# Front's masks on row halves, local scores as fp32 products without DRAM, and the last batch's networks by halves, under a new static order

## What is computed

```python
scores = jnp.einsum('bhqd,bhkd->bhqk', q, k) * scale       # Front: heads of 8, q and k rotated
attn = softmax(scores + causal_mask);  out = attn @ v @ Wo.T
...
gate = fp4_linear(x, w_gate);  y = fp4_linear(x, w_up)      # ffn: 128 -> 352 -> 128
return fp4_linear(silu(gate) * y, w_down)                   # both operands quantised in blocks of 16
...
att = jnp.einsum('bghqd,bghkd->bghqk', q, k) * scale        # local: 32-row windows
att = softmax(where(causal, att, -max));  y = att @ v @ w_proj
```

## Time and profile before

| | |
|---|---|
| median of 3 runs | 486.38 us (483.7 to 489.49) |
| the profiled execution, whole | 487.43 us |
| its span, first to last instruction | 485.6 us |
| TensorE busy | 372.8 us (77%), 4405 products |
| VectorE busy | 308.1 us (63%) |
| ScalarE busy | 205.2 us (42%) |
| Pool busy | 160.1 us (33%) |
| mean granted TensorE clock | 0.812 |
| DMA | 29.5 MB in 58736 packets, queues 25% busy |
| chain that ended last | PE 49%, DVE 25%, ACT 11%, POOL 7% |

### The profile page before, as it was taken

The page is one execution under the profiler, slowest core; times in us unless marked ns, Lnnn a source line. Parts: engine busy times, 40 slices in busy tenths (PEclk is TensorE's granted clock), DMA queues, the critical chain, the costliest instruction groups (busy, mean ns, idle before and its releaser), DMA issues.

```text
span 485.6 us, 10900 instructions
## 1 busy us (share of the span) xinstructions
PE 372.8 (77%) x4405; PEld 211.9 (44%) x4405; DVE 308.1 (63%) x698; ACT 205.2 (42%) x556; POOL 160.1 (33%) x250
## 2 busy tenths in 40 slices
PE   3175987897899789788986988899899766856333
PEld 2041353263347346453754464547536523623213
DVE  3885066438616988867796778688876676435350
ACT  2123432535444384457444724574454632522100
POOL 1201042226114344624263426335341533422202
PEclk9676576677769799979998999799979967855655
DMA  6444014006401532505050503331040031040000
GB/s 199 137 94 90 12 47 84 1 1 154 108 3 34 99 98 50 116 12 131 27 108 13 130 3 93 50 106 29 12 131 2 14 106 26 14 113 19 11 1 11
DMA packets 58787, 30.23 MB, mean 62 GB/s; under 512 B 3248, under 2 KB 58352, under 8 KB 58736
## 3 DMA queue, kind: packets, MB, share of 16 engines
q1 hardware_dynamic: 58736, 29.52, 24.9%
HBM read 15.88 MB, written 13.63 MB: 61 GB/s over the span
## 4 chain that ended last, share of the span: by engine, by line
PE 49%; DVE 25%; ACT 11%; POOL 7%; issue 5%; SPq 2%; DMA 1%; POOLq 0%; ACTq 0%; DVEq 0%
PE banks L903 9%; DVE bmax L1311 6%; PE banks L801 6%; PE banks L790 4%; PE banks L788 4%; PE banks L703 4%; PE banks L784 3%; PE banks L916 3%; ACT prob L987 3%; PE banks L862 3%; PE banks L772 2%; PE banks L911 2%; PE banks L830 1%; POOL fb__w L1138 1%; DVE nmaxl L1354 1%
## 5 line engine op out<-in xcount | busy, mean ns | idle before, releaser
L987 ACT ACTIVATE prob<-banks 128x384 f32<-128x384 f32 x128 | 56.0, 488 | 30.9 <-PE banks L790 30.7
L1311 DVE TENSOR_REDUCE bmax<-banks 128x6 f32<-128x768 f32 x64 | 59.1, 953 | 6.0 <-PE banks L772 5.3
L903 PE MATMUL banks<-wguT,fb__xqT 128*128 128x352 f32 x64 | 31.0, 621 | 6.5 <-DVE fb__h L1388 5.0
L801 PE MATMUL banks<-prob,Vf 128*32 128x128 f32 (+1 forms) x512 | 34.6, 399 | 0.6 <-ACT oTf L935 0.6
L1387 DVE SCALAR_TENSOR_TENSOR fb__hg<-fb__th,banks 128x352 f32<-128x352 f32 x16 | 8.3, 520 | 38.1 <-ACT fb__th L1058 38.1
L1138 POOL TENSOR_TENSOR fb__w<-fb__w,fb__c 128x704 f32<-128x704 f32 x8 | 13.4, 1671 | 53.0 <-DVE fb__w L1267 53.0
L784 PE MATMUL banks<-Qf,Kf 48*128 48x256 bf16 x128 | 20.1, 310 | 12.8 <-ACT prob L987 9.3
L790 PE MATMUL banks<-maskb,identb 128*128 128x256 bf16 x128 | 29.0, 314 | 0.0
L1138 POOL TENSOR_TENSOR fa__w<-fa__w,fa__c 128x704 f32<-128x704 f32 x8 | 13.4, 1672 | 45.6 <-DVE fa__w L1267 45.6
L903 PE MATMUL banks<-wguT,fa__xqT 128*128 128x352 f32 x64 | 27.2, 554 | 1.6 <-ACT fa__xqT L935 1.2
L772 PE MATMUL banks<-maskb,identb 128*128 128x256 bf16 x128 | 27.9, 304 | 0.0
(11 more groups left out here) (209 smaller groups left out, 915.7 us busy)
## 6 DMA issues: line engine op xcount, KB each, us to landing
scr_f<-partsf SPq DMA_DIRECT2D x16, 192.0 KB, 2.3
Qf<-scr_f SPq DMA_DIRECT2D x16, 192.0 KB, 3.5
Kf<-scr_f SPq DMA_DIRECT2D x16, 192.0 KB, 4.6
scr_l<-partsl SPq DMA_DIRECT2D x16, 192.0 KB, 2.2
Ql<-scr_l SPq DMA_DIRECT2D x16, 192.0 KB, 3.3
Kl<-scr_l SPq DMA_DIRECT2D x16, 192.0 KB, 4.1
scr_f<-partsf SPq DMA_DIRECT2D x16, 128.0 KB, 1.9
scr_l<-partsl SPq DMA_DIRECT2D x16, 128.0 KB, 1.9
```

The source lines that it names most:

```text
L801: mm = pe.matmul(bank[3][32 * j:32 * j + 32, k * P:SEQ], Vf[:, k, h, :], prob[:, h % 8, 256 * k:256 + 128 * k], start=(k == 0), stop=(k == ...
L903: mm = pe.matmul(bank[6 + m][:, 0:I], w.xqT[:, t * P:(t + 1) * P], wguT[:, m, :], start=True, stop=True)
L987: act.activation(prob[:, h % 8, :], bank[h % 3][:, 0:384], ACT.Exp).then_inc(f.s_exp, 1)
L1311: dve.tensor_reduce(bmax[:, 2 * g:2 * g + 2, :], banks[:, first:first + 2, 0:384].rearrange("p h (n k) -> p h n k", k=P), AX.X, ALU.max).t ...
```

## The change

1. *Row halves.* The mask is no longer one product of 128 rows for each head. The new `put_masks` adds it as two products of 64 rows for each head (output rows 0 to 63 and 64 to 127), even heads from partitions 0 to 63 and odd heads from 64 to 127, as the score products lie. The part of the mask that is zero is left out (128 + 64 columns per block instead of 128 + 128). The maxima product takes 64 rows (24 with content, the rest zero) instead of 24.
2. *Local scores.* q and k stay fp32 and are not split or sent through DRAM. `Ql` is a copy of the transposed q. `Kl` holds, for each window and each group of four heads, k four times, each time multiplied by a 0/1 column that keeps one head's 8 rows (`headsl`): diagonal blocks, so that one product over 32 rows with 128 columns gives the scores of four heads. ScalarE writes `Kl` in four copies, in batches 6 and 7 VectorE in one operation. The scores come in two halves of 16 products, the second after a wait for the first (`l_half`), each after its half of the mask. The products of q's heads are placed by another reordering of `wvb` and `wprojb`.
3. *Last batch.* For batch 7, both networks use banks 0 to 3 instead of turns on 6 and 7; gate/up of the second tile does not wait for the first; VectorE quantises and finishes tile by tile; Pool finishes only tile 0, VectorE tile 1; the quantised input is finished on VectorE as well.
4. *Order.* `FFN_TURNS` and the whole of `TIMES` are new. A few rows of it show less than the order it gives, which stands below.

```diff
+            def put_masks(S, first, upper, lower, signal):
+                at = first
+                for half, cols in ((0, upper), (1, lower)):
+                    n = cols.stop - cols.start
+                    for j in range(2):
+                        rows = slice(64 * j, 64 * j + 64)
+                        mm = pe.matmul(ends(S[j], cols), identb[rows, (half + j) % 2, :], maskb[rows, at:at + n].unsqueeze(1).to_broadcast([64, 2, n]),
+                                       start=False, stop=True, skip_group_check=True)
+                        if half == 1:
+                            mm.then_inc(signal, 1)
+                    at += n
...
-                maxima = [slice(64 * r, 64 * r + 3 * PAIRS) for r in range(2)]
+                maxima = [slice(64 * r, 64 * r + 64) for r in range(2)]
...
-                    for j in range(2):
-                        pe.matmul(ends(ring4(2 * g + j)), identb[:, :], mask_qk, start=False, stop=True, skip_group_check=True).then_inc(f.s_sc_ps, 1)
+                    put_masks([ring4(2 * g + j) for j in range(2)], 0, slice(0, P), slice(64, P), f.s_sc_ps)
...
-                        for j in range(2):
-                            pe.matmul(ends(ring(2 * g + j)), identb[:, :], mask_kq, start=False, stop=True, skip_group_check=True).then_inc(f.s_st_ps, 1)
+                        put_masks([ring(2 * g + j) for j in range(2)], P + 64, slice(0, 64), slice(0, P), f.s_st_ps)
...
-            def local1(b):
-                yield
-                scatter(b, l, partsl, scr_l)
-                yield
-                if b > 1:
-                    sp.wait_ge(l.s_sc_ps, b - 1)
-                fetch(b, l, scr_l, Qls[b % 2], Kls[b % 2])
-                yield
...
+                for c in range(2):
+
+                    if c == 1:
+                        yield
+                        pe.wait_ge(l_half, b + 1)
+                    blocks = [bank[4 + r].rearrange("p (t c k) -> p t c k", t=T, c=2)[:, :, c, :] for r in range(2)]
+                    for r in range(2):
+                        pe.matmul(blocks[r], identb[:, 0, :], mask_loc.rearrange("p (t c k) -> p t c k", t=T, c=2)[:, :, c, :],
+                                  start=(c == 0), stop=True, skip_group_check=True)
+                    for t in range(T):
                         for n in range(P // LS):
-                            k0, c0 = t * P + n * LS, (t * PAIRS + g) * LS
+                            w = t * (P // LS) + n
                             for r in range(2):
-                                rows = slice(64 * r, 64 * r + NSTACK)
-                                mm = pe.matmul(bank[4 + r][n * LS:(n + 1) * LS, c0:c0 + LS], Ql[rows, g, k0:k0 + LS],
-                                               Kl[rows, g, k0:k0 + LS], start=False, stop=True, skip_group_check=True)
-                mm.then_inc(l.s_sc_ps, 1)
+                                rows = slice(LS * (2 * c + r), LS * (2 * c + r) + LS)
+                                mm = pe.matmul(blocks[r][n * LS:(n + 1) * LS, t, :], Ql[rows, w * LS:(w + 1) * LS],
+                                               Kl[rows, w, :, :].rearrange("p j k -> p (j k)"), start=False, stop=True, skip_group_check=True)
+                    mm.then_inc(l_half if c == 0 else l.s_sc_ps, 1)
...
-                copy(partsl[:, 0, :, :].rearrange("p a t -> p (a t)"), bank[4]).then_inc(l.s_part[0], 1)
-                yield
-                act.wait_ge(l.s_rest, b + 1)
-                copy(partsl[:, 1, :, :], restl[:, :, :]).then_inc(l.s_part[1], 1)
+                copy(Ql[:, :], bank[4][:, 0:SEQ]).then_inc(l.s_part[0], 1)
+                if b not in LATE:
...
+                    for j in range(4):
+                        ins = act.activation(Kl[:, :, j, :], k, ACT.Copy, scale=headsl[:, j:j + 1])
+                    ins.then_inc(l.s_part[1], 1)
...
+            def last_ffn2(w):
+                b = LAST
+                link = linker(w.s_chain2)
+                for t in range(T):
+                    yield
+                    product(link, w, b, t, bank[2 * t], bank[2 * t + 1])
+                    yield
+                    dve.wait_ge(w.s_h_ready, T * b + t + 1)
+                    yield from quantise_h(link, w, slice(t * I, (t + 1) * I))
```

620 lines of the change are left out of this document (339 added, 281 removed), and 67 rows, old and new, of tables (FFN_TURNS, TIMES).

## The result

After takes 437.0 us (median of 4, 436.7 to 438.0) against 486.8 us before (median of 4 on the same chip, 483.7 to 489.5): ratio 0.898, 95% interval 0.893 to 0.904. The profiled execution took 436.65 us, its span 434.8. The forecast was 456 us with 438 to 474: right in sign, 19 us too high, and 1 us outside the range on the side of rival 2.

The account below looks back on a forecast made before the run. It saw a dense part paced by VectorE in Front's first loop and a ScalarE-TensorE ring in the second, then a tail of waiting chains. 487.4 - 18.5 (Front's end) - 13 (tail) = 456 us, range 438 to 474.

Parts of the forecast that it names:

- rival 2: Whole kernel: TensorE bounds the dense part throughout, so row halves, moved work and tail gain more; 441 us, chance 0.12.
- The ring step: Front's second loop: product to next exponential 0.74 us for 0.86, exponential to exponential 1.28 us for 1.40.
- What the row halves are worth: Front's loops: masks and maxima on 64 rows save 11 us in the second loop and 3 in the first.
- The new order: Dense part: work moved behind Front's last projection or out of its steps ends Front 5 us earlier.
- The local scores: Dense part: ScalarE's extra copies cost 2 us, the dropped VectorE subtraction gains 1.5; TensorE loses nothing to 1.1 a batch.
- The end: Tail from Front's last addition: 90 us for 103, from +2, -6 and -9.
- the 97: Sign of being wrong: Front's last addition to the end stays over 97 us.
- (a): Tail, Front's end to local batch 7's transposed q and k: 50 us for 48, +2.
- (b): Tail, local batch 7 from transposes to maxima: 8 us for 14.85 without the DRAM path, -6 net.
- (c): Tail, last network by halves: -9 us, its end within 21 us of the last local addition.
- Rival 1: Dense part gains only 6 us, as VectorE, ScalarE or the static order absorbs it; about 474 us, chance 0.18.
- Rival 3: Dense part: thinner TensorE work drops the granted clock from 0.93 to 0.73; near 509 us, chance 0.05.

Follow-up runs that it names:

- e15: After with the maxima back on 24 rows, masks still on row halves: 457.2 us (449.8 to 459.3).
- e1: Before with only the row halves (masks and maxima on 64 rows), in its own order: 461.6 us, beside 485.1 for before on the same chip.
- e5: After without the row halves (128-row masks, 24-row maxima): 449.9 us (449.7 to 452.6), beside 483.5 for before on the same chip.
- e4: Row halves, local scores and last-batch halves together, in before's order: 465.2 us (457.4 to 465.3).
- e8: e4 with Kl built by one VectorE product in every batch, none by ScalarE: 453.2 us (451.5 to 462.4).
- e14: The kernel of e8 unchanged, on the chip of e13: 457.3 us (451.0 to 462.4).
- e9: After once more, unchanged, five more timed executions: 433.4 us (429.9 to 437.7).
- e6: After with the mask products of Front's second loop made twice: 440.7 us (439.0 to 442.1).
- e7: After with the mask products of Front's first loop made twice: 433.9 us (432.9 to 434.3).
- e13: e8 with local batch 5's second half, local network 4 and network 6's down moved behind Front's end: 468.7 us (465.1 to 470.1).
- e10: After with local network 6's last down product behind the last network's up products, its addition as late: 436.4 us (431.4 to 437.0).
- e3: Before with only the last batch's networks by halves, in before's order: 481.1 us (479.6 to 481.7).
- e11: After with products that nobody reads ahead of TensorE's waits in the last 50 us: 436.9 us (433.3 to 437.9).
- e12: After with the edits of e7, e10 and e11 together: 431.7 us (429.4 to 433.8).

## Why the prediction was wrong where it was

**The ring step: right.** 0.74 forecast, 0.70 measured, down from 0.86. The bare period fell from 1.40 to 1.24 to 1.25 us, 1.28 forecast. The price of 0.10 us per change of row tiling was about right: two changes and what hangs on them cost 0.21 us in e15 (0.91 against 0.70). ScalarE's idle before the exponentials is 20.7 us, about 22 forecast. The mask's weights still show "issue" idle, but 3.9 us in 512 loads; e15 has 15.1.

**What the row halves are worth: right between like executions, 14 us forecast, 13 in e1.** In after's order they are worth 13 to 20 us (e5). e1 has four executions only, so a faster one may be missing and the 13 may be too little. e1's median is 23.5 us below before's and its Front's end 23.8 earlier, which looks like rival 2's 64 x (0.23 + 0.15) = 24. That figure does not hold: only 13 of the 34.7 us of TensorE time are left when the clock is taken out, and 14.4 us of the earlier end lie in the four second loops that before ran below the full clock. How the 13 us divide between the ring and TensorE's queue, and between the two loops, is not shown.

**The new order: the large miss, 5 us forecast, 27 between the fastest of e4 and after.** The failed step is that I costed only what the order put behind Front's end, "I take 5". What it moves within Front's part had no term. About 6 us are ScalarE's four copies of Kl, which left the second loops (e8, e14). The forecast booked 2 us for them as a cost of the local scores, with 4.2 as the most: it counted the copies' own length, which was about right (1.56 us for four), and not what waits behind them.

The other 21 us stand between e14 (451.6 us, clock 0.89) and e9 (430.4, 0.87). Here are e14's sums over the eight batches, then e9's: first loops (first score product to last maximum), what lies between the two loops, and second loops (first transposed score product to last exponential).

```profile
sum 88.51, PE 61.69 PEld 39.80 DVE 81.94 ACT 31.04 POOL 42.26; mean PE 7.71 PEld 4.98 DVE 10.24 ACT 3.88 POOL 5.28
sum 38.20, PE 28.96 PEld 17.68 DVE 24.92 ACT 20.66 POOL 9.48; mean PE 3.62 PEld 2.21 DVE 3.12 ACT 2.58 POOL 1.18
sum 106.93, PE 92.99 PEld 49.99 DVE 65.86 ACT 77.60 POOL 29.78; mean PE 11.62 PEld 6.25 DVE 8.23 ACT 9.70 POOL 3.72
```

```profile
sum 76.85, PE 61.64 PEld 39.92 DVE 71.35 ACT 32.80 POOL 29.17; mean PE 7.71 PEld 4.99 DVE 8.92 ACT 4.10 POOL 3.65
sum 23.94, PE 10.49 PEld 6.00 DVE 20.56 ACT 8.17 POOL 4.00; mean PE 1.31 PEld 0.75 DVE 2.57 ACT 1.02 POOL 0.50
sum 124.43, PE 113.59 PEld 63.13 DVE 71.59 ACT 90.72 POOL 40.46; mean PE 14.20 PEld 7.89 DVE 8.95 ACT 11.34 POOL 5.06
```

- *Between the loops* 14.3 us are gone, with 18.5 us of TensorE work of other stages. In the old order such work stands there in TensorE's order. In e14's batch 6 `nmTf`, the input of the second loop, is copied by 285.53, and the loop starts at 289.69, behind a network's and a local stage's products:

```profile
285.04 0.49 ACT L995 ACTIVATE nmTf<-banks 128x384 bf16<-128x384 bf16 x1
285.32 2.55 PE L936 MATMUL banks<-wguT,fa__xqT 128*128 128x352 f32 x4
287.67 1.40 PE L855 MATMUL banks<-wqkvb,xnTl 128*128 128x256 f32 x4
289.69 0.28 PE L810 MATMUL banks<-Qf,Kf 48*128 48x256 bf16 x2
```

- *The first loops* are 11.7 us shorter with the same TensorE time (61.7 and 61.6) and 10.6 us less VectorE time: what left them is VectorE's work for other stages, and VectorE paces them (busy 81.9 of 88.5 us, then 71.4 of 76.8). TensorE's wait for the maxima falls with it (18.9 us in e4, 7.9 in after).
- *From a last exponential to the next batch's first product*, the start included, it is 11.0 us less (109.5 to 98.5), and the last such piece, up to Front's end, 2.1 less.
- *The second loops* took up what left, and are 17.5 us longer with 20.6 us more TensorE time. Behind Front's end TensorE is busy 13 us more (54.4 to 67.4), and that part is only 0.7 us longer.

So the order does not empty the second loops, it fills them: other stages' work went from places where Front stands still into loops in which it has to wait anyway. e6 and e7 show that more TensorE work in a loop costs less than its length there, and e13 that the move behind Front's end alone costs 7 to 14 us in the old order. How the 21 us divide among these moves is read from the traces only; a version with one of them alone was not run.

**The local scores: mis-sized in one part.** Forecast 0.5 us worse at Front's end. e14, with Kl on VectorE, has Front's end 2.8 us earlier than e1 at a like clock. e4, with ScalarE's copies, is 4.1 us faster than e1 between the fastest, and its part behind Front's end is 7.6 us shorter (95.8 for 103.4), which leaves Front's end some 3.5 us later, an estimate. So the exchange itself is a small gain, and ScalarE's copies ate it. On TensorE nearly nothing changed, as taken: 256 products, two records of 274 ns for each, 10.7 us for 9.7 before.

**The forecast's sum.** Between the fastest executions the three parts in the old order gain 17 us (474.4 to 457.4), where the forecast had 28.5 for them (14 for the row halves, -0.5 for the local scores, 6 and 9 behind Front's end), and the order 27, where it had 5 less 2. So the 19 us by which the forecast missed are not one error but two of opposite sign, and that it missed by no more is luck.

**The end: 13 us forecast, 6 measured.** The distance from Front's last addition to the end is 99.3 us, over the 97 that I had named as a sign of being wrong (96.5 in e9's profile). (a) was 2 us for the local part of batch 7: its addition comes 72.4 us behind Front's end, as before (452.60 - 380.24), although (b) held: the timeline of after has

```profile
384.06 0.42 DVE L1426 TENSOR_TENSOR xall<-banks,xall 128x256 f32<-128x256 f32 x1 [0.92 <-PE banks L916]
384.63 0.66 PE L716 MATMUL banks<-identf,xnl 128*128 128x128 f32 x2 [0.61 <-DVE xall L1426]
...
392.81 0.60 PE L716 MATMUL banks<-identf,qkn 128*128 128x128 f32 x4
393.45 0.38 ACT L994 ACTIVATE Ql<-banks 128x256 f32<-128x256 f32 x1 [1.46 <-PE banks L716]
...
398.03 1.29 DVE L1418 TENSOR_REDUCE nmaxl<-banks 128x16 f32<-128x512 f32 x2 [0.43 <-PE banks L888]
399.14 1.02 PE L894 MATMUL banks<-nmaxl,identf 128*128 128x512 f32 x2
```

5.7 us from the copy of the transposed q (393.45) to the added maxima, where 8 were forecast and 14.9 stood before, with no wait for a DMA. So (a) is the step that failed here: I took q and k of local batch 7 as transposed at 50 us behind Front's end, and they were at 58.0 (393.45). Network a7 was done at 36.3 where I had 34; the rest is the line of the local batches. Batch 7's first transposes stand behind local batch 6's addition (the first two rows), as they did before (420.78 and 421.35), and that addition now comes 48.6 us behind Front's end instead of 40.6. The clock is not the reason: it was 0.89 in these 49 us, and 0.80 in before's first 48 us behind Front's end. The other profile of after (e9) has that addition at 46.0 us. (c) forecast 21 us from the last local addition to the last addition, and it took 24.4 (407.90 to 432.30):

```profile
413.94 1.36 PEld L948 LDWEIGHTS banks<-wdT,fb__hqT 128*128 128x128 f32 x6 [1.06 <-ACT fb__hqT L994]
415.39 0.63 PE L716 MATMUL banks<-identf,fb__xq 128*128 128x128 f32 x2
423.87 0.93 POOL L606 TENSOR_TENSOR fb__w<-fb__w,fb__c 128x352 f32<-128x352 f32 x1 [12.61 <-DVE fb__w L1323]
425.71 0.47 PEld L970 LDWEIGHTS banks<-identf,fb__u 128*128 128x128 f32 x3 [5.20 <-POOL fb__u L608]
430.61 1.65 PE L975 MATMUL banks<-wdT,fb__hqT 128*128 128x128 f32 x6 [0.63 <-ACT fb__hqT L994]
432.30 0.29 DVE L1487 TENSOR_TENSOR xall<-banks,xall 128x128 f32<-128x128 f32 x1 [3.06 <-PE banks L975]
```

Its input was ready at 413.85 and stood behind network 6's last product until 415.18. I had written that this product falls behind, and had charged it to the local part; it cost the last network 1.3 us (e10's profile has 1.4 to 2.2 less there). The same halves in before's order took 22.8 us (e3).

**The rivals.** Rival 1 (small gain) fell with e1. Rival 2 was nearest, 441 us, by luck: its 24 us for the row halves are not borne out at a like clock, its 15 for the tail were 6, and its 7 for the order were as wrong as my 5. Rival 3's clock did not fall: 0.95 from 157 us to Front's end, where it was 0.93 to 380 us. Of the Trainium skill's rule (TensorE: Matmul & The Clock Gate, "Part 3: Packing small matmuls — row/col tiling"), that a load overlaps products only on another row group, after again shows the other side: the second pair of score products starts 0.12 us behind the first, on the same rows, with its loads beside them (193.22, 0.10 us, while the first pair runs until 193.49).

## What to carry to other kernels

Price a change in a hand-written order by the place that the work leaves and the place that it enters: cut the longest chain into its loops and the pieces between them, sum each engine's busy time in each, and look for other stages' work that stands in a piece where the chain has nothing to wait for. Compare only executions or loops at a like granted clock: a gain of 13 us looked like 24 here. Work put behind the end of the longest stage is not free when a chain of later batches starts from it. And when products are cut to fewer rows, look at the row count of their neighbours in the same step before counting the gain: the cut alone can lose.

## What the runs showed of the hardware that was not expected

- A change of row tiling between neighbouring products showed as 0.16 to 0.17 us of "issue" idle before the next weights (e15, both changes of the step shown). The Trainium skill (TensorEngine Tiling (Array Packing), "Key Properties") says that changing the tiling mode drains TensorE; the trace is in line with it, and gives the size.
- A ScalarE copy of 256 columns with a scale per partition takes 487 ns, a plain one 383. Four in a row start 0.36 us apart (1.56 us in all, e4).
- The same program ran from 429.9 to 437.7 us with mean granted clocks of 0.884 and 0.856 (e9). Between the two profiles (428.6 and 434.8 us) 4.3 us lie in the second loops, batch 5's alone having 14.7 us at 1.00 and 17.2 at 0.80, and 2.9 behind Front's end.
- Products that nobody reads, put into TensorE's waits, came with a higher granted clock there (0.98 for 0.64 in one stretch of 8 us, e11), and the end from the last local addition on was 1.9 to 2.6 us shorter, although TensorE had more to do. With e10's edit as well (e12) it was only 0.7 to 1.4 us shorter.
